# The stacked keys of the first attention issued in two halves, earlier, with the maxima's rows between them

## The reference

```
x = x + tanh(g_xattn[0]) * L0_xattn(layernorm(x), ctx, ctx)   # the first attention
x = x + tanh(g_ffn[0])   * L0_ffn(layernorm(x))
x = x + tanh(g_xattn[1]) * L1_xattn(layernorm(x), ctx, ctx)
x = x + tanh(g_ffn[1])   * L1_ffn(layernorm(x))

# L0_xattn: 16 heads of 16 channels, two softmaxes per head
s1 = (q wq1)(k wk1)^T / 4 ;  s2 = (q wq2)(k wk2)^T / 4
attn = softmax(s1) - gain * softmax(s2)
o = attn (v wv);  o = (o - mean) / sqrt(var + eps)  per head;  out = o wo^T
```

## Time and profile before

| | |
|---|---|
| time before, median of 3 runs | 1793.35 us (1788.36 to 1796.01) |
| the profiled execution's own time | 1810.53 us |
| its span, first to last instruction | 1808.4 us |
| mean granted TensorE clock | 0.876 |
| PE busy in the span | 1503.6 us, 83% |
| DVE, ACT, POOL busy | 1277.4, 1117.2, 614.6 us |
| stack_keys' DMAs | 192 of 256 KB, median 8.8 to 9.0 us from issue to landing |

### The profile page before, as it was taken

The page is one execution under the profiler, slowest core; times in us unless marked ns, Lnnn a source line. Parts: engine busy times, 40 slices in busy tenths (PEclk is TensorE's granted clock), DMA queues, the critical chain, the costliest instruction groups (busy, mean ns, idle before and its releaser), DMA issues. The chain is left out here.

```text
span 1808.4 us, 31323 instructions
## 1 busy us (share of the span) xinstructions
PE 1503.6 (83%) x11798; PEld 1011.7 (56%) x11798; DVE 1277.4 (71%) x2552; ACT 1117.2 (62%) x1938; POOL 614.6 (34%) x559
## 2 busy tenths in 40 slices
PE   3899999989999999999993787888757998837686
PEld 2566666656566666666661455555545676623275
DVE  3466667665767775676445899998633799989875
ACT  1365556555666665576444777777634575669996
POOL 1044444443535353444323322231110445563100
PEclk9588879886989997899656999999977999969999
DMA  6536455363754563554402000000043222028399
GB/s 143 83 56 94 66 83 83 57 93 45 104 76 67 91 83 56 71 81 69 55 2 70 1 1 1 1 1 1 13 128 93 57 77 63 25 85 334 143 370 374
DMA packets 103153, 153.61 MB, mean 85 GB/s; under 512 B 10934, under 2 KB 83766, under 8 KB 96834
## 3 DMA queue, kind: packets, MB, share of 16 engines
q1 hardware_dynamic: 102716, 151.62, 38.4%
q10 hardware_dynamic: 288, 0.00, 0.0%
HBM read 65.80 MB, written 33.95 MB: 55 GB/s over the span
## 5 line engine op out<-in xcount | busy, mean ns | idle before, releaser
L625 DVE TENSOR_REDUCE neg_max<-psum 128x8 f32<-128x1024 f32 x256 | 313.1, 1223 | 181.4 <-PE psum L413 179.0
L544 ACT ACTIVATE exp_t<-psum 128x512 f32<-128x512 f32 x512 | 278.1, 596 | 128.7 <-PE psum L425 128.4
L425 PEld LDWEIGHTS psum<-q_stack,k_stack 50*128 50x128 f32 x2048 | 156.7, 216 | 94.2 <-issue 79.9
L708 POOL TENSOR_TENSOR sq<-u 128x256 f32<-128x256 f32 x64 | 39.2, 613 | 497.1 <-DVE u L642 497.1
L425 PE MATMUL psum<-q_stack,k_stack 50*128 50x128 f32 x2048 | 195.5, 316 | 0.3 <-ACT exp_t L544 0.2
L413 PE MATMUL psum<-k_stack,q_stack 48*128 48x256 f32 x1024 | 148.5, 373 | 55.8 <-issue 42.4
L436 PE MATMUL psum<-exp_t,v_pad 128*32 128x256 f32 x2048 | 189.9, 448 | 0.0
L716 POOL TENSOR_TENSOR rs<-rs,minus_half 128x16 f32<-128x16 f32 x64 | 187.0, 2921 | 5.0
L549 ACT ACTIVATE o_t<-psum 128x512 f32<-128x512 f32 x128 | 76.6, 598 | 143.8 <-PE psum L436 143.5
L413 PEld LDWEIGHTS psum<-k_stack,q_stack 48*128 48x128 f32 x1024 | 90.9, 218 | 118.5 <-issue 110.7
L533 ACT ACTIVATE q_stack<-psum 128x512 fp32r<-128x512 f32 x128 | 75.5, 590 | 87.7 <-PE psum L401 87.5
(11 more groups left out here) (209 smaller groups left out, 3351.2 us busy)
## 6 DMA issues: line engine op xcount, KB each, us to landing
k_stack<-k_hi SPq DMA_DIRECT2D x128, 256.0 KB, 8.8
g_scratch<-f_gelu SPq DMA_DIRECT2D x24, 1024.0 KB, 3.9
f_gelu<-g_scratch SPq DMA_DIRECT2D x24, 1024.0 KB, 14.8
k_stack<-k_lo SPq DMA_DIRECT2D x64, 256.0 KB, 9.0
x_state<-in_x SPq DMA_DIRECT2D x8, 1024.0 KB, 11.0
ctx_t<-in_ctx_t SPq DMA_DIRECT2D x64, 128.0 KB, 2.3
a_ctx_g<-in_ctx_t SPq DMA_DIRECT2D x32, 256.0 KB, 3.3
a_kt<-in_ctx_t SPq DMA_DIRECT2D x64, 128.0 KB, 2.3
```

Source lines behind the costliest of these rows:

```text
L425: r = e.matmul(psum[:, 2 + j, o:o + P], self.k_st[rows, b // 2 % self.NK, pair % 4, b % 2, pair // 4, i, :], self.q_st[rows, b % self.NQ, ...
L544: e.activation(self.prob[:, n % 3, j].rearrange("p n w t -> p (n w t)"), psum[:, 2 + j, :], ACT.Exp).then_inc(s["exp"], 1)
L625: e.tensor_reduce(self.negm[:, b % 2, :, :, 2 * u:2 * u + 2].rearrange("p j w n -> p j n w"), psum[:, 0:2, :].rearrange("p j (n w k) -> p ...
```

## The change

`stack_keys(p, h)` now stacks one half h of the channels for both slots, in six DMAs of 128 KB, so a pair has twelve. The half 0 is issued at tick 16p-18 and the half 1 at 16p-12, instead of everything at 16p-10. By this `max_rows(2p-3)` (16p-13) stands between the two halves on SP, and `load_context(p+1)` (16p-10) comes behind the second half instead of ahead of the first. Each half waits only for its own half of k_lo and k_hi. Of the scores three pairs before, the half 0 waits for the second unit (st_pe two lower than before), the half 1 for all. The axes of k_hi, k_lo and k_stack are swapped so that a half is one run of 512 elements (2 KB), and `k_landed` waits for 192.

```diff
@@ k_landed
-        w.wait_ge(self.s_kdma[p % self.NK], 96 * (p // self.NK + 1))
+        w.wait_ge(self.s_kdma[p % self.NK], 192 * (p // self.NK + 1))
@@ sp
-        def stack_keys(p, j):
+        def stack_keys(p, h):
             k = p % self.NK
-            w.wait_ge(s["k_lo"], 2 * p + 2)
-            w.wait_ge(s["k_hi"], 2 * p + 2)
+            w.wait_ge(s["k_lo"], 2 * p + h + 1)
+            w.wait_ge(s["k_hi"], 2 * p + h + 1)
             w.wait_ge(s["one_rows"], 208)
-            w.wait_ge(s["st_pe"], 8 * (p - self.NK + 1))
-            for part, src in ((0, self.k_hi), (1, self.k_lo), (2, self.k_hi)):
-                r = SLOT * j + HD0 * part
-                e.dma_start(self.k_st[r:r + HD0, k].rearrange("e t s h w k -> e t (s h w k)").bitcast(F32),
-                            src[SLOT * j:SLOT * j + SLOT, p % 2].rearrange("p s h w k -> p (s h w k)").bitcast(F32)
-                            ).then_inc(self.s_kdma[k], 16)
+            w.wait_ge(s["st_pe"], 8 * (p - self.NK + 1) - 2 + 2 * h)
+            for j in range(2):
+                for part, src in ((0, self.k_hi), (1, self.k_lo), (2, self.k_hi)):
+                    r = SLOT * j + HD0 * part
+                    e.dma_start(self.k_st[r:r + HD0, k, :, h].rearrange("e t s w k -> e t (s w k)").bitcast(F32),
+                                src[SLOT * j:SLOT * j + SLOT, p % 2, h].rearrange("p s w k -> p (s w k)").bitcast(F32)
+                                ).then_inc(self.s_kdma[k], 16)
...
-            if (tick + 10) % 16 == 0 and 0 <= (tick + 10) // 16 < NSEQ // 2:
-                stack_keys((tick + 10) // 16, 0)
-                stack_keys((tick + 10) // 16, 1)
+            if (tick + 18) % 16 == 0 and 0 <= (tick + 18) // 16 < NSEQ // 2:
+                stack_keys((tick + 18) // 16, 0)
+            if (tick + 12) % 16 == 0 and 0 <= (tick + 12) // 16 < NSEQ // 2:
+                stack_keys((tick + 12) // 16, 1)
@@ maxima (scores_t in the same way)
-                                 self.k_st[rows, b // 2 % self.NK, pair % 4, b % 2, pair // 4].rearrange("p w k -> p (w k)"), start=True, stop=True)
+                                 self.k_st[rows, b // 2 % self.NK, pair % 4, pair // 4, b % 2].rearrange("p w k -> p (w k)"), start=True, stop=True)
@@ k_high on ScalarE (rest_keys on VectorE in the same way)
-            e.activation(self.k_hi[:, p % 2, :, h].rearrange("p s w k -> p s (w k)"), psum[:, 4, :].rearrange("p (s c) -> p s c", s=2),
+            e.activation(self.k_hi[:, p % 2, h].rearrange("p s w k -> p (s w k)"), psum[:, 4, :],
                          ACT.Copy).then_inc(s["k_hi"], 1)
```

More of the change, by code:

```diff
@@ L327, in sp @@
                     r = SLOT * j + MROW
-                    e.dma_start(self.k_st[r:r + 2, i, 2 * k:2 * k + 2].rearrange("p t s h w k -> p (t s h w k)").bitcast(F32),
+                    e.dma_start(self.k_st[r:r + 2, i, 2 * k:2 * k + 2].rearrange("p t h s w k -> p (t h s w k)").bitcast(F32),
                                 self.ones_zeros).then_inc(s["one_rows"], 16)
@@ L425, in scores_t @@
                         r = e.matmul(psum[:, 2 + j, o:o + P],
-                                     self.k_st[rows, b // 2 % self.NK, pair % 4, b % 2, pair // 4, i, :],
+                                     self.k_st[rows, b // 2 % self.NK, pair % 4, pair // 4, b % 2, i, :],
                                      self.q_st[rows, b % self.NQ, pair, :], start=True, stop=True)
@@ L615, in rest_keys @@
         def rest_keys(p, h):
-            flat = lambda z: z[:, p % 2, :, h].rearrange("p s w k -> p s (w k)")
+            flat = lambda z: z[:, p % 2, h].rearrange("p s w k -> p (s w k)")
             w.wait_ge(s["k_hi"], 2 * p + h + 1)
-            e.tensor_tensor(flat(self.k_lo), psum[:, 4, :].rearrange("p (s c) -> p s c", s=2), flat(self.k_hi).bitcast(F32),
+            e.tensor_tensor(flat(self.k_lo), psum[:, 4, :], flat(self.k_hi).bitcast(F32),
                             ALU.subtract).then_inc(s["k_lo"], 1)
```

## The result

The changed kernel takes 1,658.86 us (median of 4 runs, 1,651.03 to 1,669.07) against 1,793.15 us: a ratio of 0.9257, 95% interval 0.9201 to 0.9312. The forecast was 1,653 us, range 1,628 to 1,705. The profiled execution took 1,669.07 us, so its rows stand beside the 1,810.53 us of the profiled execution before.

A forecast was written before the change was run, and what follows sets the result against it. TensorE was taken to be held up by late keys in the first attention, its clock falling behind the waits. Pairs −138.6, end −13.4, start 0: 1,810.5 to 1,658.5, less 6 for execution differences: 1,653 us, range 1,628 to 1,705.

The forecast's parts named there:

- The bound: First attention: TensorE waits for the stacked keys before L413, 24 waits, 42.4 us in all, and its clock falls behind them.
- The rival in which the low clock has another reason: First attention: only the waits go, the low-clock stretches stay; 1,745 us, chance 0.07.
- The pairs: L413 of pair 3 to that of pair 31: 28 pairs at 23.13 us instead of 28.1, −138.6 us.
- The end of the stage: First attention from 903.92 to 941 us: 37.08 us at clock 0.50 become 23.7, −13.4 us.
- The start: First pairs: later context of pair 1 adds 4.4 us, a wait of 4.2 us goes; nothing in sum.
- the second wait: Start, 4.16 us before L413 at 63.63: goes, as the halves of pair 1 are issued earlier, −4.2 us.
- Six us were taken off: Whole run: 35% of the 17.2 us between profiled execution and median, taking 1,658.5 to 1,653 us.
- The queue price of a half: Stacking DMAs: a half takes 6.5 us of queue if bytes count, 13.1 us if pieces count; 6.5 taken.
- The estimate from the Trainium skill's table: Stacking DMAs: 128 KB cost 0.65 of 256 KB, making a half 8.5 us; no term of the sum.
- The late context: Rival: context lands late, keys matmul waits up to 1 us; 1,681 us, or 1,715 with clock falls; chance 0.14.
- the rival in which pieces count: Stacking DMAs: 2 KB pieces hold engines as long as 4 KB ones, 26.2 us queue per pair; 1,860 us, chance 0.04.
- 13.1 us per pair: Stacking DMAs: queue time of a pair's 1.5 MB at 120 GB/s, 6.5 us per half if bytes count.

The follow-up runs named there:

- e6_before_filled: The kernel before, with two additional filler matmuls per pair on TensorE ahead of the wait for the keys: 1,718.40 us, ratio 0.9521.
- e2_both_ahead: The changed kernel with both halves issued at tick 16p−14, ahead of the maxima's rows, each by its own wait: 1,655.99 us, ratio 0.9175.
- e11_best: The changed kernel with the context of pair 1 loaded first at the start and the second half at tick 16p−14: 1,694.89 us, ratio 0.9383.
- e13_twelve_of_4k: The kernel before, each of its six stacking DMAs cut in two by partitions, twelve of 128 KB in 4 KB pieces: 2,235.53 us, ratio 1.2442.

## Why the prediction was right, and where not

**The bound.** That TensorE waited for the keys' landing was right: the waits are gone with nothing else changed on TensorE. That the wait lets the clock fall was right, and is now shown and not only read, by e6_before_filled, in which the keys are as late as before and the clock stays up. The rival in which the low clock has another reason is out. What the Trainium skill says of the clock ("TensorE: Matmul & The Clock Gate", section HAM oscillation) would have kept it up at waits of 1.3 to 2.4 us; the traces do not agree.

**The sum.** The pairs: −138.6 forecast, −141.95 measured, since a pair took 23.07 us for the 23.13 of the earlier trace rows and the last, without any further keys to make, 21.34. The end of the stage: −13.4 forecast, −13.93 measured. The start: 0 forecast, +4.05 in the profile; the context held TensorE up for 5.85 us (first L415 +3.6 us, for +4.4), and the second wait went, as forecast, but the pairs behind it ran at a low clock for 44 us, so what the second wait gave back was lost. In the repeat of the change pair 3 began at 116.66, so the start is −1 to +4. For the profiled execution the sum gave 1,658.5, measured were 1,669.07: the pairs and the end brought 3.9 us more than forecast, the start 4.05 less, and the parts behind L201, in which nothing changed, took 10.4 us more. Six us were taken off for how executions differ; the profile of the change is 10.2 us above its median. So the forecast of 1,653 for 1,658.86 rests on a right account of the pairs; that it came within 6 us is in part luck, since the start and the parts behind L201 alone move an execution by more.

**Landings.** Forecast and measured, ahead of L415: first half 18 and 18.0; second half 9.3 and 9.1; context 8.3 and 8.3, wanted at 5.7. The queue price of a half, 6.5 us by bytes, measured some 6.2 (8.4 from first issue to last landing, less the 2.2 of the earlier trace rows). The estimate from the Trainium skill's table ("DMA: Bandwidth & Descriptors", section Bandwidth), 8.5, does not hold here: the halving was no loss. The late context, but for the start of the program, and the rival in which pieces count are out.

**What failed.** Not a number but the account of what each part of the change is for. The prediction costed the split at nothing for itself and laid the gain on the place. The runs show that the split alone, at the old place, brings the time to 0.934 where the whole change brings it to 0.926, and 115 of the 142 us of the 28 pairs. Two steps were behind this: "13.1 us per pair" for both ways, where twelve DMAs of 2 KB pieces took 14.2 us from first issue to last landing and six with 4 KB 15.3; and the loss by the clock, which was reckoned for waits that stay or go whole, where it depends on the wait's length: 19 waits of 1.8 us brought the clock to 0.85, 22 of 0.8 us left it at 0.99. The forecast of the whole change was untouched, as it took all waits away. And in e2_both_ahead and e11_best I had read ticks as times.

**Open.** Whether the quicker landing comes of the smaller piece, as the packets suggest, or of the smaller DMA; e13_twelve_of_4k changed the spread as well. The old DMAs of 256 KB at an earlier place were not tried, so what the place gives without the split is not known.

## What to carry to other kernels

A stall of 2 us that recurs costs more than 2 us when TensorE's clock falls behind it: price such a stall from two stretches of the trace, one with it and one without, and test the parts of the remedy apart: here waits of 0.8 us in place of 1.8 were already four fifths of the gain. A large transfer on a queue delays every small one issued behind it: cut it at the small transfer that is wanted soonest, and let each part go by its own wait. In an order written by ticks, ask which semaphore releases a DMA and what stands ahead of it on its queue, not how many ticks it was moved.

## What the runs showed of the hardware that was not expected

- Short idle stretches of TensorE, when they recur, lower its clock: 16 waits of 2.4 us in 650 us gave 0.77, 19 of 1.8 us 0.85, 22 of 0.8 us 0.99, and 1.00 with two matmuls of filler before the wait, which left 14 waits of 0.5 us.
- Six DMAs of 256 KB between on-chip tiles took 15.3 us from first issue to last landing (median), twelve of 128 KB with pieces of 2 KB 14.2 us at the same place and 14.7 to 14.8 at two others; twelve with 8 target partitions and 32 pieces of 4 KB kept the DMA engines half busy (share 0.5, 60 GB/s).
- A small DMA issued behind a full queue waits for all that is ahead of it and lands close behind: 7.4 us from issue for the maxima's rows, 0.4 us after the last of twelve large ones; a context load that found the queue empty took 2.2 us.
